# Grouped attention of a four-layer stack on Trainium2: scores as two rounded products, four batches as one stream, inverses and normalising by pairs

## The reference

```python
h = _rms(x, ln_w)
q = (h @ wq).reshape(B, S, 32, 64)
k = (h @ wk).reshape(B, S, 8, 64)
v = (h @ wv).reshape(B, S, 8, 64)
q, k = _rope(q, k)
k = jnp.repeat(k, 4, axis=2)
v = jnp.repeat(v, 4, axis=2)
scores = jnp.einsum('bqhd,bkhd->bhqk', q, k) / np.sqrt(64)
scores = jnp.where(causal, scores, -1e30)
o = jnp.einsum('bhqk,bkhd->bqhd', softmax(scores, -1), v).reshape(B, S, 2048)
x = x + o @ wo
```

## Time and profile before

| | us |
|---|---|
| median of 3 runs | 3048.33 (3042.65 to 3050.93) |
| profiled execution, whole | 3039.91 |
| profiled execution, span | 3038.1 |
| PE busy in the span | 2452.8 (81%) |
| DVE, ACT, POOL busy | 1693.3, 1243.7, 1324.6 |
| mean granted clock of TensorE | 0.909 |

### The profile page before, as it was taken

The page is one execution under the profiler, slowest core; times in us unless marked ns, Lnnn a source line. Parts: engine busy times, 40 slices in busy tenths (PEclk is TensorE's granted clock), DMA queues, the critical chain, the costliest instruction groups (busy, mean ns, idle before and its releaser), DMA issues. The chain is left out here.

```text
span 3038.1 us, 44303 instructions
## 1 busy us (share of the span) xinstructions
PE 2452.8 (81%) x12088; PEld 1662.4 (55%) x12088; DVE 1693.3 (56%) x5549; ACT 1243.7 (41%) x3486; POOL 1324.6 (44%) x1245
## 2 busy tenths in 40 slices
PE   6999999938998998999899589952657485599992
PEld 6888888934555555556455466531323233277661
DVE  7666666655653662663565343328645656653334
ACT  3444444434542552553454244321445253433331
POOL 3444444414552551553454158862220302117885
PEclk9999999979999999999999789986688796889996
DMA  4000000020000000000000635550000000224554
GB/s 153 15 14 14 14 14 14 5 80 1 1 2 1 2 1 2 1 1 2 1 1 1 227 61 86 86 130 0 1 1 0 0 0 0 112 74 84 86 86 111
DMA packets 72733, 112.48 MB, mean 37 GB/s; under 512 B 11648, under 2 KB 59520, under 8 KB 72128
## 3 DMA queue, kind: packets, MB, share of 16 engines
q0 software_dynamic: 30336, 42.73, 8.7%
q1 hardware_dynamic: 37968, 63.15, 5.9%
q10 hardware_dynamic: 4224, 4.19, 0.4%
HBM read 80.69 MB, written 36.32 MB: 39 GB/s over the span
## 5 line engine op out<-in xcount | busy, mean ns | idle before, releaser
L1017 POOL TENSOR_TENSOR b_sm<-b_sm,b_rden 128x128 f32<-128x128 f32 (+3 forms) x512 | 363.4, 721 | 267.1 <-DVE b_rden L985 257.7
L927 ACT ACTIVATE b_sm<-b_sm,b_mn 128x128 f32<-128x128 f32 (+3 forms) x512 | 286.3, 559 | 349.0 <-DVE b_mn L979 349.0
L848 PEld LDWEIGHTS b_t<-ident,b_sm 128*128 128x128 f32 x1280 | 156.0, 141 | 221.1 <-issue 120.1
L839 PE MATMUL b_s<-b_k,b_q 128*128 128x128 f32 (+3 forms) x688 | 254.1, 454 | 21.8 <-POOL b_q L1004 21.8
L848 PE MATMUL b_t<-ident,b_sm 128*128 128x128 f32 x1280 | 229.7, 278 | 43.3 <-POOL b_sm L1017 30.6
L979 DVE CUSTOM_DVE_ANT_0 b_sm<-b_s,maskB 128x128 f32<-128x128 f32 (+3 forms) x344 | 167.1, 486 | 148.6 <-issue 147.7
L1380 POOL DMA_INDIRECT XN<-rows,m_slots x158 | 158.2, 1001 | 94.0 <-issue 47.6
L409 POOL TENSOR_TENSOR a_q<-a_prod 128x512 f32<-128x512 f32 x64 | 81.8, 1278 | 229.0 <-DVE a_prod L355 229.0
L1962 DVE TENSOR_REDUCE c_nm<-c_first 128x2 f32<-128x1024 f32 x128 | 149.7, 1217 | 35.1 <-PE c_first L1753 35.1
L825 PE MATMUL b_pj<-b_h,b_w 128*128 128x512 f32 x320 | 161.9, 594 | 0.0
L860 PE MATMUL b_o<-b_pt,b_v 128*64 128x512 f32 (+3 forms) x1024 | 157.3, 450 | 3.9 <-DVE b_pt L971 3.9
(11 more groups left out here) (288 smaller groups left out, 5826.7 us busy)
## 6 DMA issues: line engine op xcount, KB each, us to landing
WM<-in_m_w_dram SPq DMA_DIRECT2D x4, 3072.0 KB, 17.0
WM<-in_m_w_dram SPq DMA_DIRECT2D x4, 2432.0 KB, 14.0
acc<-in_zeros_dram SPq DMA_DIRECT2D x3, 2176.0 KB, 15.5
n_part<-acc SPq DMA_DIRECT2D x12, 512.0 KB, 7.1
a_wa<-in_a_wa_dram SPq DMA_DIRECT2D x8, 512.0 KB, 4.6
b_w<-in_b_w_dram SPq DMA_DIRECT2D x1, 3072.0 KB, 9.8
XN<-rows,m_slots POOLq DMA_INDIRECT x158, 2.8
X<-in_x_dram SPq DMA_DIRECT2D x4, 512.0 KB, 5.7
```

Of the source, the lines that this page charges most:

```text
L839: pe.matmul(p_s[g % 3][:, 0:keys(t)], q_r[:, m % 2, t * P:(t + 1) * P], kp[:, m // B_REP % 2, head, 0:keys(t)], start=True, stop=True).the ...
L848: x = pe.transpose(p_t[g % 2][:, k * P:(k + 1) * P], sm[:, g % RING, k * P:(k + 1) * P], c.ident[:, :])
L927: act.activation(sm[:, g % RING, 0:keys(t)], sm[:, g % RING, 0:keys(t)], ACT.Exp, scale=-1.0, bias=mn[:, g % RING:g % RING + 1], accum_out ...
L1017: pool.tensor_tensor(sm[:, s, 0:keys(t)], sm[:, s, 0:keys(t)], rden[:, s:s + 1].to_broadcast([P, keys(t)]), ALU.mult).then_inc(s_pn, 1)
```

## The change

- Scores: queries and keys are kept as rounded parts in the type float32r. `round_q` (ACT) writes the rounded query for both heads, `low_q` (POOL) the rest (`ql`), and `double_q` (ACT for head 0, DVE for head 1) overwrites the other head's rows with this head's query. `round_k` (ACT) and `low_k` (DVE) do the like for keys: `k_full` has the rounded keys of a head and, in the other head's rows, their rest; `k_padded` the rounded keys and zeros. An item's scores are then two products in float32r, `qh` with `k_full` and `ql` with `k_padded`, into one bank.
- Batches: the four loops are unrolled into one stream of 64 units (512 items). Projections of later keys and values go `beside` the items, values into the tensor `Y` with room for two batches. Queries are projected two units ahead. There is one projection bank instead of two, and two score banks instead of three. The copy `h` goes; PE reads `c.HT`.
- Output projection: each unit's, two units later, at items 2 and 3, into two banks that collect a batch; DVE adds them once a batch. `ot` has two buffers.
- Inverses and normalising: for the two heads of a query tile by one instruction each, at odd items on DVE and in the order `add`, `normalise`, `low_q` on POOL. `INV` is 3 and `LAG` 5.

```diff
     ITEMS = 2 * TB
-    LAG = 4
+    LAG = 5
     CLAG = LAG + 1
-    INV = 2
+    INV = 3
     RING = 8
...
+    VALUES_AT = CLAG + 1
+    COPY_AT = (VALUES_AT + 1) % ITEMS
+    UNITS = BATCH * B_UNITS
+    PAIR_COUNT = BATCH * B_PAIRS
+    TOTAL = UNITS * ITEMS
...
+    def beside(M):
+        m = M % B_UNITS
+        if M < UNITS and m % B_REP == 1 and M // B_REP + 1 < PAIR_COUNT:
+            return ("k", M // B_REP + 1, 0)
+        if M < UNITS and m in (6, 8, 10, 12) and M // B_UNITS + 1 < BATCH:
+            return ("v", M // B_UNITS + 1, (m - 6) // 2)
+        return None
...
-        v_s = sb("v", [P, TB, B_PAIRS * P])
-        q_r = sb("q", [P, 2, SEQ])
+        v_s = c.Y[:, :, :].rearrange("p (b t a) d -> p b t (a d)", b=2, t=TB)
+        k_full, k_padded = sb("k_full", [P, 2, 2, SEQ], F32R), sb("k_padded", [P, 2, 2, SEQ], F32R)
+        k_r, q_r = sb("k_rot", [P, SEQ]), sb("q_rot", [P, SEQ])
+        qh, ql = sb("q_high", [P, 2, 2, SEQ], F32R), sb("q_low", [P, 2, SEQ], F32R)
...
+        ot = sb("ot", [P, 2, SEQ])
+        p_j, p_s, p_t = pb("pj"), [pb("s0"), pb("s1")], [pb("t0"), pb("t1")]
+        p_o, p_y = pb("o"), [pb("y0"), pb("y1")]
...
+                def scores(G):
...
+                    out = p_s[G % 2][:, 0:keys(t)]
+                    pe.matmul(out, qh[:, M % 2, head, t * P:(t + 1) * P], k_full[:, pg % 2, head, 0:keys(t)],
+                              start=True, stop=False)
+                    pe.matmul(out, ql[:, M % 2, t * P:(t + 1) * P], k_padded[:, pg % 2, head, 0:keys(t)],
+                              start=False, stop=True).then_inc(s_sc, 1)
+                def transposes(G):
...
+                    pe.wait_ge(s_pn, G // 2 + 1)
+                    if G >= 2:
...
+                def out_proj(M, half):
...
+                    for t in (2 * half, 2 * half + 1):
+                        x = pe.matmul(p_y[half][:, t % 2 * DIM:(t % 2 + 1) * DIM], ot[:, M % 2, t * P:(t + 1) * P], wo[:, m, :],
+                                      start=(m == 0 and t % 2 == 0), stop=(m == B_UNITS - 1 and t % 2 == 1),
+                                      skip_group_check=True)
...
+                for G in range(LAST):
+                    M, n = G // ITEMS, G % ITEMS
+                    if G < TOTAL:
+                        scores(G)
+                    if n < 2 and beside(M) is not None:
+                        project(beside(M), n)
+                    if n in (2, 3) and 0 <= M - 2 < UNITS:
+                        out_proj(M - 2, n - 2)
+                    if n in (4, 5) and M + 2 < UNITS:
+                        project(("q", M + 2, 0), n - 4)
+                    if LAG <= G < TOTAL + LAG:
+                        transposes(G - LAG)
+                    if n == VALUES_AT and 0 <= M - 1 < UNITS:
+                        values(M - 1)
...
+                def round_q(M, head):
+                    if head == 0:
+                        act.wait_ge(s_rope, ROPES["q", M, 0] + 1)
+                        if M >= 2:
+                            act.wait_ge(s_sc, (M - 1) * ITEMS)
+                    x = act.activation(qh[:, M % 2, head, :], q_r[:, :], ACT.Copy)
+                    if head == 1:
+                        x.then_inc(s_qh, 1)
+                def double_q(M):
+                    act.wait_ge(s_ql, M + 1)
+                    act.wait_ge(s_qh, M + 1)
+                    for half in range(2):
+                        x = act.activation(qh[rows(1, half), M % 2, 0, :], q_r[rows(0, half), :], ACT.Copy)
+                    x.then_inc(s_qa, 1)
...
+                for G in range(LAST):
+                    M, n = G // ITEMS, G % ITEMS
+                    if CLAG <= G < TOTAL + CLAG and item(G - CLAG)[1] == 0:
+                        copy_pt(G - CLAG)
+                    if G < TOTAL:
+                        exp(G)
+                    if M + 1 < UNITS:
+                        if n in (1, 2):
+                            round_q(M + 1, n - 1)
+                        if n == 5:
+                            double_q(M + 1)
+                        if M % B_REP == 2 and n in (0, 3) and M // B_REP + 1 < PAIR_COUNT:
+                            round_k(M // B_REP + 1, n // 3)
+                    if n == COPY_AT and 0 <= M - 2 < UNITS:
+                        copy_out(M - 2)
...
+                def double_q(M):
+                    dve.wait_ge(s_qh, M + 1)
+                    for half in range(2):
+                        x = dve.tensor_copy(qh[rows(0, half), M % 2, 1, :], q_r[rows(1, half), :])
+                    x.then_inc(s_qd, 1)
+                def low_k(pg, head):
+                    if head == 0:
+                        dve.wait_ge(s_kh, pg + 1)
+                    for half in range(2):
+                        x = dve.tensor_tensor(k_full[rows(1 - head, half), pg % 2, head, :], k_r[rows(head, half), :],
+                                              k_full[rows(head, half), pg % 2, head, :].bitcast(F32), ALU.subtract)
...
+                def inverse(G):
+                    s = G % RING
+                    dve.wait_ge(s_exp, G + 2)
+                    dve.reciprocal(rden[:, s:s + 2], den[:, s:s + 2]).then_inc(s_rd, 1)
...
-                        if INV <= g < TOTAL + INV:
-                            s = (g - INV) % RING
-                            dve.wait_ge(s_exp, b * TOTAL + g - INV + 1)
-                            dve.reciprocal(rden[:, s:s + 1], den[:, s:s + 1]).then_inc(s_rd, 1)
...
+                for G in range(LAST):
+                    M, n = G // ITEMS, G % ITEMS
+                    if CLAG <= G < TOTAL + CLAG and item(G - CLAG)[1] == 1:
+                        copy_pt(G - CLAG)
+                    if G < TOTAL:
+                        minimum(G)
+                    if G % 2 == 1 and INV <= G < TOTAL + INV:
+                        inverse(G - INV)
+                    if n == 2 and beside(M) is not None:
+                        read(beside(M))
+                    if n in (6, 7) and M + 2 < UNITS:
+                        read(("q", M + 2, 0), n - 6)
+                    if n == 4 and M + 1 < UNITS:
+                        double_q(M + 1)
+                    if M % B_REP == 3 and n in (1, 3) and M // B_REP + 1 < PAIR_COUNT:
+                        low_k(M // B_REP + 1, n // 2)
+                    if n == 5 and M >= 2 and (M - 2) % B_UNITS == B_UNITS - 1:
+                        add_y((M - 2) // B_UNITS)
...
+                def add(job, dst):
...
+                    pool.tensor_tensor(dst[:, :], prod[:, 0, :], prod[:, 1, :], ALU.add).then_inc(s_rope, 1)
+                def low_q(M):
+                    pool.wait_ge(s_qh, M + 1)
+                    pool.tensor_tensor(ql[:, M % 2, :], q_r[:, :], qh[:, M % 2, 0, :].bitcast(F32),
+                                       ALU.subtract).then_inc(s_ql, 1)
+                def normalise(G):
+                    _, _, t = item(G)
+                    s = G % RING
+                    pool.wait_ge(s_rd, G // 2 + 1)
+                    pool.tensor_tensor(sm[:, s:s + 2, 0:keys(t)], sm[:, s:s + 2, 0:keys(t)],
+                                       rden[:, s:s + 2].rearrange("p (s o) -> p s o", o=1).to_broadcast([P, 2, keys(t)]),
+                                       ALU.mult).then_inc(s_pn, 1)
...
+                for G in range(TOTAL):
+                    M, n = G // ITEMS, G % ITEMS
+                    if n == 0 and M + 1 < UNITS:
+                        add(("q", M + 1, 0), q_r)
+                    if n % 2 == 0:
+                        normalise(G)
+                    if n == 1 and M + 1 < UNITS:
+                        low_q(M + 1)
+                    if n == 2 and beside(M) is not None and beside(M)[0] == "k":
+                        add(beside(M), k_r)
```

More of the change, by code:

```diff
@@ L750, in attention1 @@
     ITEMS = 2 * TB
-    LAG = 4
+    LAG = 5
     CLAG = LAG + 1
-    INV = 2
+    INV = 3
     RING = 8
[L755 to L768, removed]
+    VALUES_AT = CLAG + 1
[3 more added lines that the diff above has]
+    TOTAL = UNITS * ITEMS
+    LAST = TOTAL + 2 * ITEMS
+    def beside(M):
[5 more added lines that the diff above has]
+        return None
+    order = [("v", 0, t) for t in range(TB)] + [("k", 0, 0), ("q", 0, 0), ("q", 1, 0)]
+    for M in range(UNITS):
+        if beside(M) is not None:
+            order.append(beside(M))
+        if M + 2 < UNITS:
+            order.append(("q", M + 2, 0))
+    LOADS = {job: at for at, job in enumerate(order)}
+    ROPES = {job: at for at, job in enumerate(job for job in order if job[0] != "v")}
     with ExitStack() as st:
@@ L812, in _, with project @@
             def _(pe):
[L813 to L818, removed]
+                def project(job, part=None):
+                    kind, i, t = job
+                    at = LOADS[job]
+                    if part != 1 and at > 0:
+                        pe.wait_ge(s_prod, at)
+                    b = {"v": i, "k": i // B_PAIRS, "q": i // B_UNITS}[kind]
@@ new lines, in copy_out @@
```

(28 more changed lines are left out.)

288 lines of the change are left out of this document (116 added, 172 removed).

## The result

The kernel after takes 3149.1 us in the median of 4 runs (3147.1 to 3151.0), against 3047.7 for the kernel before: ratio 1.034, 95% interval 1.033 to 1.035. It is slower by 101 us; the forecast was 3060, with a range up to 3125.

What follows compares the result with a forecast made beforehand. The order of DVE, ACT and POOL, not TensorE's sum, was taken to bound the kernel. 64 units of 14.5 us plus 98 us made 1026 against 1014, +12 us on 3048.3: 3060 us, range 2945 to 3125.

Steps and rivals of the forecast that it cites:

- the removed scores: Score products on TensorE: two rounded products replace the plain one, 4.30 to 2.58 us, 1.72 us a unit, 110 us over 64.
- two waits of PE a unit: TensorE standing for ACT's transposed copies: before the transposes of step 3, 1.7 to 2.4 us, and before the unit's last transposes.
- ACT idle 2.60 before `round_q`: ACT at step 1: forecast to idle some 2.5 us a unit, until POOL's `add` of the next query ends.
- fill 32.5 (33), tail 11.5 (11): Ends of the single stream: first fill forecast at 33 us, drain of the last unit at 11 us.
- Step 6: DVE's `double_q` at step 4, held behind POOL's `low_q`: copies end at 8.95 us held, 7.85 or 8.4 not held.
- the terms of TensorE's work: One unit's scores, transposes, `values`, query and output projections on TensorE: 2.58 + 2.2 + 2.31 + 1.72 + 1.72, given as 10.55 us.
- rival C: TensorE's clock falls to half: 5.6 us a unit; with three in ten units 108 us, 3168 us; chance 0.07.
- The sign named for it: Profile after: granted clock 0.95 or more from 715 us to the stage's end; prediction wrong if below 0.9.
- The unit: Spacing of `values` in the edited stage: 14.5 us with DVE's copies held, 13.6 or 13.9 not, times 64.
- the walk's links from step 1 to step 7: One unit followed through PE, DVE, POOL and ACT from the previous `values`, with handover times between engines, ending at 14.5 us.
- The bound of +/-30 us: The forecast's own range from the bounds of handovers and keys: 3030 to 3090 us.
- The keys: Each of 15 key projections: 0.86 us TensorE, 0.2 ACT, 2.0 DVE `low_k`, 3.1 taken of 2.0 to 4.3, 47 us.

Runs made afterwards that it cites:

- e9: Kernel after with each score as one plain product of the rounded values, the query's lower part left out of the scores: 3121.1 us (1.024).
- e7: Kernel after with DVE's `double_q` alone moved from step 4 to step 6: 3082.9 us (1.013).
- e5: Kernel after with 1.29 us of unused matmuls in PE's wait ahead of a unit's last transposes: 3118.0 us (1.024).
- e14: Kernel after with pairs kept but one item earlier, inverse 2 items after the pair's first minimum and transposes at a lag of 4: 2976.9 us (0.978).
- e10: One plain product per score, query's lower part left out, in the 2954 us kernel with queues mended and key work spread: 3016.9 us (0.991), 63 us more.
- e1: Kernel after with POOL's `add` of the next query ahead of the unit's last normalising: 3104.9 us (1.019).
- e18: Kernel after with ACT's two `round_q` at steps 2 and 3 instead of 1 and 2: 3205.9 us (1.052).

## Why the prediction was wrong

The bound was read right: the order of three engines, not TensorE's sum. So were these steps: the removed scores bring nothing (e9: less than nothing); two waits of PE a unit, ended by ACT's copy (1.42 and 1.59, walked 1.7 to 2.4 and 1.4, so the first over-priced); ACT idle 2.60 before `round_q` (2.5); the pair of 512 at 1.89 (1.90); products at their rounded pace; fill 32.5 (33), tail 11.5 (11). Step 6, the held copy, was decided right and, for a plain unit, priced right: e7 gave 0.98 for 0.9, but 0.55 in the mean over all units. The Trainium skill (page "SBUF — State Buffer", section "Who interferes with whom") has such a cast and a GpSimd operation shut each other out, and the traces agree: 0.42 us alone, 0.99 in the mean beside a POOL operation. In the unit shown the two casts took 1.09 and 0.42, and the first ended 0.28 us after `low_q`.

One slip of addition changed nothing: the terms of TensorE's work sum to 10.53, not 10.55. On the profiled execution's own basis the miss is 3150 less 3052, 98 us. Three terms make it up (100 by these counts): two that the sum had too small, and one that it put at nothing. Without either of the first two below the time, 3149, would have been inside the range that ended at 3125.
- **The clock, rival C, 33 us (put at nothing).** It was set aside because PE worked 10.5 of 14.5 us and rows 8 showed one wait with the clock kept. That was a failed step: one wait in a stretch where PE works 93% says nothing about two in every unit. It was also priced as all or nothing (5.6 us a unit, three units in ten). What came is a third of the units at 1.5 us each (e5: 31 us back). The sign named for it could not show this: the mean granted clock from 715 to 1800 us is 0.96, inside the "0.95 or more" of the forecast, because the falls stand where all engines wait for PE.
- **The unit, 15.32 for 14.5, 52 us over 64 (mis-sized).** This is the largest term, and the other failed step: the walk's links from step 1 to step 7 were mis-sized. No wait was missed; nearly every link was somewhat longer. The handover of a rounded product to DVE costs 0.11 more; to the end of minimum(5) 0.14; exp(5), `double_q` and copy on ACT 0.40 (two `double_q` are 1.27, not 1.04; from the start of exp(5) to theirs, with the read-out of its sum, it is 0.62); ACT to PE 0.05; the last transposes 0.12. The bound of +/-30 us on "handovers and keys" was less than half of the 67 us that this term and the next came to.
- **The keys, 4.1 us each for 3.1, 15 us.** The three units around one take 17.70, 15.58 and 16.83 in e5, against 15.33. Within the bounds given (2.0 to 4.3), at their upper side: `low_k` is 1.17 us in the mean.

The walk was of the kernel as written, so the lag of 5 is in its waits and is no part of the miss. But it never walked the same unit at a lag of 4, and so did not say which part of the change costs. The runs do: with inverse and transposes one item earlier the time is 156 to 172 us less, and all the rest of the change together is a gain of 65 (e14's 2976.9 against 3041.7 for the kernel before, run beside it).

## What to carry to other kernels

In an in-order queue, walk where each copy that frees a bank stands against every wait on the same engine; a lag changed by one item flips odd and even steps; here lag and inverse together moved some 170 us, slow `values` included. Price a wait of TensorE with the clock that it may take from the work right behind it, and try filling it with unused matmuls: if that makes the kernel faster, the clock is part of the cost. Look at the clock by microsecond around the work that others wait for, not at its mean over the stage. When an edit removes TensorE work and PE is found waiting, first mend the queue; the same products cost 28 us in one order (e9) and gained 63 in the other (e10).

## What the runs showed of the hardware

TensorE's granted clock fell to 0.50 (1.2 GHz) during the `values` behind a wait of 1.59 us in 22 of 64 units of the kernel after, in 44 with the same wait and the earlier one gone (e1), and in 52 when two waits stood together (e18); units with the same 1.59 us kept it. With 1.29 us of unused matmuls in that gap it was 1.00 during all `values`, and 0.50 for 41 us at other places (e5). A DVE cast of 32x512 to the rounded type is 0.42 us alone, but two of them took 1.52 beside one POOL operation and 2.03 beside the end of `low_q` and a normalising (e14), and that normalising of 768 columns took 1.70 us, not 1.47. Engines that had only to wait, as POOL before an early addition, passed the delay on to whatever stood behind them.
